# A Mamba scan stage: the C product of every third tile's ninth unit moves from GpSimd to VectorE

## The chip, the cores and the metric

The kernel runs on one core of a Trainium2 chip. The metric is the device time of one execution in microseconds (us). The core has TensorE (PE, whose weight loads are listed apart as PEld), VectorE (DVE), ScalarE (ACT), GpSimd (POOL) and SyncE (SP, which here only issues DMA transfers). The engines run side by side, each through its own list of instructions in order, and wait for each other through counting semaphores.

## The reference

The reference is one layer of a gated cross-attention block whose "attention" is a Mamba selective scan, followed by a mixture of experts. The change touches only the scan. Cut to that:

```python
u = silu(conv(in_proj(ctx)) + conv_b)               # 4 batches x 1024 channels x 1024 times
delta = softplus(dt_proj(x_proj(u)[:32]) + dt_b)
Bm, Cm = ...                                        # 16 states each, shared by all channels
def step(state, xs):                                # over time
    d_t, B_t, C_t, u_t = xs
    dA = exp(d_t[..., None] * A)
    state = state * dA + (d_t * u_t)[..., None] * B_t[:, None, :]
    y_t = einsum('ben,bn->be', state, C_t)
    return state, y_t
y = y + D * u
y = y * silu(layernorm(x))
x = x + tanh(g_xattn) * y
```

After it come the routing of tokens, 32 experts and a shared expert, which the change leaves alone.

## The kernel before

`program` runs five stages one after the other: `mamba_inputs`, `selective_scan`, `shared_pass` (part 0), `experts`, `shared_pass` (part 1). All data is f32.

`selective_scan` works through NU = 32 **channel tiles** (4 batches x 8 tiles of 128 channels; tile i belongs to batch i // 8). A tile has NST = 16 **units**, one for each state n. A unit, numbered k = 16 i + n, is a 128 x 1024 array, channels by time. For one unit each engine does one step, and each walks the 512 units in the same order:

- TensorE, `multiply_b(k)` (L1021, 8 matmuls): delta times u times B into the one PSUM buffer `psb`. It waits until ScalarE has emptied `psb` of unit k-1 (`s_ev`).
- ScalarE, `copy_input` (L951): copies `psb` to SBUF (`dbu`, groups of four units, two groups). It does this three units ahead (AHEAD), right after the exponential of unit k.
- ScalarE (L958): the decay exp(delta * A) into PSUM `da[k % 2]`. It waits until VectorE's scan of unit k-2 is done (`s_scan`, count k-1), since that scan read the same buffer.
- VectorE (L983), `tensor_tensor_scan`: the state over time, from `da` and `dbu` into one of the four slots of `h` in SBUF. It waits for its decay, for all four copies of its group, and until TensorE has read the slot's last content (`s_ys`).
- GpSimd (L1000): multiplies the slot in place by C (`c[:, n]`, one of 16 resident rows), and raises `s_hc`.
- TensorE, `add_state(k)` (L1031, 8 transposing matmuls): adds the product into PSUM `psy`, the tile's sum over the states. In TensorE's list it stands after `multiply_b(k + 6)` (BEHIND). Units 6 to 9 also carry the D * u term (L1040).

When the tile's 16 units are summed, VectorE's `gate_tile` (L975) multiplies `psy` by the gate and by silu. It stands in VectorE's list after the scan of unit 1 of the *next* tile (GATED), and TensorE may begin the next tile's sum only after it (`s_gated`). SyncE stores the result and loads what the following tiles need; at the turn of a batch (tiles 8, 16, 24) it also loads the new B matrices `m0`, `m1` and the 16 rows of C, each behind a wait for the last reader.

VectorE and GpSimd are joined by `s_scan` one way and, through TensorE's transposes and the four slots of `h`, by `s_ys` the other way.

Of the kernel before, what the change touches and what calls it, by code (L numbers as in the profile page):

```python
# [8 lines left out]
DI, NST, DR, DC = 1024, 16, 32, 4  # L9
# [5 lines left out]
ET = DI // P  # L15
# [13 lines left out]
GN = 4  # L29
# [5 lines left out]
ALU = mybir.AluOpType  # L35
# [8 lines left out]
def after(eng, sem, value):  # L44

    if isinstance(value, int):
        if value > 0:
            eng.wait_ge(sem, value)
    else:
        assert value.min_val > 0  # L50
        eng.wait_ge(sem, value)
# [726 lines left out]
def selective_scan(nc, io, dr, ident, arena, m0, duT, early):  # L778
# [4 lines left out]
    with ExitStack() as ctx:  # L783
        sb = lambda name, shape, dt=F32: ctx.enter_context(nc.sbuf_tensor(name, shape, dt))
        sem = Semaphores(nc, ctx)
        NU = B * ET
        SETS = NU * NST
        PARTS = 4
        CP = NC // PARTS
        HR = 4  # L790
        AHEAD, BEHIND = 3, 6
        GATED, SKIPPED = 1, 6
        skip = sb("skip", [P, P])
        gate = sb("gate2", [P, 1])
        m0, m1 = m0[:], sb("m", [P, TB * ROW], F32R)[:]
        m = [v.rearrange("p (t c n) -> p t c n", t=TB, c=NC) for v in (m0, m1)]
        c = sb("c", [P, NST, L])
        ad = sb("ad", [P, 2, NST + 1])
        dl = sb("dl", [P, 2, L])
        dbu = sb("dbu", [P, 2, GN, L])  # L800
        h = sb("h", [P, HR, L])
        aux = sb("aux", [P, ET, P])
        da = [ctx.enter_context(nc.psum_tensor(f"da{i}", [P, L], F32)) for i in range(2)]
# [9 lines left out]
        s_cl = [sem(f"p2_c_loaded{n}") for n in range(NST)]  # L813
# [6 lines left out]
        s_da = sem("p2_decay")  # L820
        s_scan = sem("p2_state")
        s_hc = sem("p2_state_times_c")
        s_ys = sem("p2_summed")
        s_sk = sem("p2_skip_matrix")
        s_skip = sem("p2_skip_added")
# [4 lines left out]
        def units(body):  # L830
            for i in range(NU):
                for n in range(NST):
                    body(i, n, i * NST + n)

        @block.sync
        def _(sp):
# [21 lines left out]
                    sp.dma_start(dst_, src_).then_inc(s_m[half], 16)  # L858

            def load_c(b, n):  # L860
                after(sp, s_hc, (b * ET - 1) * NST + n + 1 if b else 0)
                sp.dma_start(c[:, n], dr["c"][b, n].partition_broadcast(P)).then_inc(s_cl[n], 16)

            def load_u(i):
# [31 lines left out]
            for n in range(3):  # L896
                load_c(0, n)
            load_m(0, 1)
            for n in range(3, NST):
                load_c(0, n)  # L900

            for i in range(NU):
                b = (i + 1) // ET
# [7 lines left out]
                if turned:  # L911
                    for n in range(8, 12):
                        load_c(b, n)
# [55 lines left out]
        @block.vector  # L969
        def _(dve):  # L970
            def gate_tile(i):

                dve.wait_ge(s_szl, i * 16 + 16)
                dve.wait_ge(s_ys, i * NST + NST)
                dve.scalar_tensor_tensor(out=aux[:], in0=psy[:], scalar=gate[:, 0:1], in1=aux[:],  # L975
                                         op0=ALU.mult, op1=ALU.mult).then_inc(s_gated, 1)

            def unit(i, n, k):
                dve.wait_ge(s_da, k + 1)
                dve.wait_ge(s_ev, (k // GN) * GN + GN)  # L980

                after(dve, s_ys, k - HR + 1)
                dve.tensor_tensor_scan(h[:, k % HR, :], da[k % 2][:, :], dbu[:, (k // GN) % 2, k % GN, :], 0.0, ALU.mult,  # L983
                                       ALU.add).then_inc(s_scan, 1)
                if n == GATED and i:
                    gate_tile(i - 1)

            dve.wait_ge(s_gate, 1)
            units(unit)
            gate_tile(NU - 1)  # L990

        @block.gpsimd
        def _(pool):
            pool.memset(f32(m1), 0.0).then_inc(s_zero, 1)

            def unit(i, n, k):
                if i % ET == 0:
                    pool.wait_ge(s_cl[n], (i // ET) * 16 + 16)
                pool.wait_ge(s_scan, k + 1)
                pool.tensor_tensor(h[:, k % HR, :], h[:, k % HR, :], c[:, n, :], ALU.mult).then_inc(s_hc, 1)  # L1000

            units(unit)

        @block.tensor
        def _(pe):
            def multiply_b(k):

                i, g, r = k // NST, (k % NST) // GN, k % GN
                if g == 0:
                    if i:  # L1010
                        pe.wait_ge(s_du[r], i * 64)
                    elif r == 0:
                        pe.wait_ge(early["du"], 64)
                half = k % (ET * NST) // NH
                if k == 0:
                    pe.wait_ge(early["m"], 2 * TB // BAND * 16)
                elif k % (ET * NST) in (0, NH):
                    pe.wait_ge(s_m[half], (i // ET + half) * 2 * TB // BAND * 16)
                after(pe, s_ev, k)
                for j in range(CP):  # L1020
                    mm = pe.matmul(psb[:, j], duT[:, r * CP + j, :], m[g // 2][:, :, r * CP + j, g % 2 * GN:(g % 2 + 1) * GN], start=True, stop=True)  # L1021
                mm.then_inc(s_mm, 1)

            def add_state(k):

                i, n = k // NST, k % NST
                if n == 0:
                    after(pe, s_gated, i)
                pe.wait_ge(s_hc, k + 1)
                for t in range(ET):  # L1030
                    mm = pe.matmul(psy[:, t, :], h[:, k % HR, t * P:(t + 1) * P], ident[:], is_transpose=True,  # L1031
                                   start=(n == 0 and t % 4 == 0), stop=(n == NST - 1 and t % 4 == 3))
                mm.then_inc(s_ys, 1)
                if n == SKIPPED:
                    pe.wait_ge(s_sk, i + 1)
                    pe.wait_ge(s_ut, i * 16 + 16)
                if 0 <= n - SKIPPED < ET // 2:

                    for t in (2 * (n - SKIPPED), 2 * (n - SKIPPED) + 1):
                        mm = pe.matmul(psy[:, t, :], ut[:, t * P:(t + 1) * P], skip[:], start=False, stop=False)  # L1040
                    if n == SKIPPED + ET // 2 - 1:
                        mm.then_inc(s_skip, 1)

            for k in range(SETS + BEHIND):
                if k < SETS:
                    multiply_b(k)
                if k >= BEHIND:
                    add_state(k - BEHIND)
# [968 lines left out]
```

## Time and profile before

| | us |
|---|---|
| time, median of 3 runs | 4216.48 |
| the 3 runs | 4215.31 to 4220.93 |
| the profiled execution, its own time | 4213.03 |
| its span (first to last instruction) | 4211.3 |
| scan stage: first scan to last gate, in the trace | 552.1 to 1785.1 |
| GpSimd busy in the whole span | 1799.1 (43%) |
| VectorE busy | 3031.8 (72%) |
| TensorE busy | 3847.6 (91%) |

Shares of the whole span average over five stages with different limits. The scan stage is some 1233 us, 29% of the span, and in it GpSimd is busy nearly without a break, which the overall 43% hides. The timeline view lists instructions of one engine in order of time and merges equal neighbours into one row; idle time below about 0.15 us inside a row is not printed. Records of neighbouring instructions of VectorE or GpSimd may overlap by up to 0.09 us, so a pace is read from start to start.

### The profile page before, as it was taken

Reading aid. Unit: us, or ns where it says so; the run is one execution under the profiler, and the core shown is the slowest. Engines: PE = TensorE matmul, PEld = TensorE weight load, DVE = VectorE, ACT = ScalarE, POOL = GpSimd, SP = SyncE. Lnnn points to the kernel's source line nnn. Section 1 sums busy time; section 2 is a strip of 40 time slices with the busy share of each in tenths; the row PEclk is TensorE's granted clock in tenths of the full one; section 3 lists DMA queues with packets and bytes.
Section 4 is the critical chain, followed back from the end, with each engine's and each line's share of the span. In section 5 each row is a group of like instructions: output and inputs, shape, how many; then the busy total and the mean of one; then the engine's idle time right before and its main releaser. Section 6 shows DMA issues by size and latency. Waiting matters only on the chain. (4 is left out here: it accounts for less than half of the span.)

```text
span 4211.3 us, 59482 instructions
## 1 busy us (share of the span) xinstructions
PE 3847.6 (91%) x21088; PEld 3151.6 (75%) x21088; DVE 3031.8 (72%) x3701; ACT 2150.4 (51%) x2257; POOL 1799.1 (43%) x1010
## 2 busy tenths in 40 slices
PE   8888378888888888869999989999999999999999
PEld 4444268888778888758888868888888888788887
DVE  7878579999999999867777755555555555455555
ACT  3677678989888889722222234444444444300000
POOL 0355279999999999923333320000000000122221
PEclk9998589999999999979999989999999999999999
DMA  6675753463453553445555557666666666677643
GB/s 231 233 274 224 256 192 108 136 183 116 140 172 116 161 154 113 138 170 175 174 183 184 189 191 245 233 236 232 235 233 234 233 236 238 220 269 262 204 161 121
DMA packets 330294, 821.67 MB, mean 195 GB/s; under 512 B 65872, under 2 KB 111696, under 8 KB 320784
## 3 DMA queue, kind: packets, MB, share of 16 engines
q1 hardware_dynamic: 298240, 752.23, 52.0%
q0 software_dynamic: 31744, 67.23, 5.3%
q8 instruction: 104, 1.70, 0.2%
q14 instruction: 62, 0.51, 0.0%
q10 hardware_dynamic: 144, 0.00, 0.0%
HBM read 603.38 MB, written 245.27 MB: 202 GB/s over the span
## 5 line engine op out<-in xcount | busy, mean ns | idle before, releaser
L1000 POOL TENSOR_TENSOR h<-h,c 128x1024 f32<-128x1024 f32 x512 | 1205.4, 2412 | 33.8 <-DVE h L983 30.8
L983 DVE TENSOR_TENSOR_SCAN h<-da,dbu 128x1024 f32<-128x1024 f32 x512 | 1134.5, 2272 | 67.6 <-ACT dbu L951 51.6
L958 ACT ACTIVATE da<-dl,ad 128x1024 f32<-128x1024 f32 x512 | 588.7, 1150 | 80.7 <-DVE h L983 67.4
L1031 PE MATMUL psy<-ident,h 128*128 128x128 f32 x4096 | 561.4, 281 | 46.1 <-POOL h L1000 26.8
L951 ACT ACTIVATE dbu<-psb 128x1024 f32<-128x1024 f32 x512 | 523.0, 1021 | 61.8 <-PE psb L1021 50.6
L1916 DVE TENSOR_TENSOR wsp<-arena,wsp 128x2048 fp32r<-128x2048 f32 x198 | 447.6, 2288 | 99.9 <-ACT wsp L1869 99.7
L1031 PEld LDWEIGHTS psy<-ident,h 128*128 128x128 f32 x4096 | 446.8, 143 | 79.7 <-POOL h L1000 52.0
L1755 POOL DMA_INDIRECT xg<-scratch_xn,ids x64 | 63.5, 992 | 1034.1 <-PE psT L1773 1010.7
L1869 ACT ACTIVATE wsp<-arena 128x2048 fp32r<-128x2048 f32 x198 | 370.9, 1910 | 24.2 <-DMA arena<-in_w 24.0
L1021 PE MATMUL psb<-m,du_taps 128*128 128x128 f32 x2048 | 288.9, 288 | 62.8 <-ACT dbu L951 62.8
L1021 PE MATMUL psb<-m_first,du_taps 128*128 128x128 f32 x2048 | 292.2, 291 | 47.1 <-ACT dbu L951 22.6
L1021 PEld LDWEIGHTS psb<-m,du_taps 128*128 128x128 f32 x2048 | 251.5, 193 | 99.8 <-ACT dbu L951 94.6
L1021 PEld LDWEIGHTS psb<-m_first,du_taps 128*128 128x128 f32 x2048 | 258.8, 198 | 78.1 <-issue 39.0
L1280 POOL DMA_INDIRECT scratch_tab<-tok_s,si_s x128 | 125.4, 980 | 444.9 <-DVE si_s L1578 398.7
L1442 ACT ACTIVATE hT_s<-psH_s 128x512 fp32r<-128x512 f32 x64 | 38.4, 599 | 503.9 <-PE psH_s L1392 485.5
L426 PE MATMUL psX<-arena 128*128 128x512 f32 x512 | 231.9, 605 | 11.2 <-DMA arena<-in_ctxT 11.2
L759 POOL TENSOR_TENSOR lbuf<-lbuf,ebuf 128x1024 f32<-128x1024 f32 x32 | 75.5, 2361 | 343.3 <-DVE ebuf L693 343.3
L1782 PE MATMUL psO<-wsp,hT 128*128 128x512 f32 x512 | 213.8, 418 | 2.1 <-DVE ob L1927 2.1
L1782 PE MATMUL psG<-wsp,xT_place 128*128 128x512 f32 x512 | 203.0, 397 | 4.9 <-DVE wsp L1916 4.9
L1855 ACT ACTIVATE xT_place<-psT 128x512 fp32r<-128x512 f32 x128 | 76.6, 598 | 250.3 <-PE psT L1773 250.3
L1783 PE MATMUL psO<-wsp,hT 128*128 128x512 f32 x512 | 202.3, 395 | 0.0
L1782 PE MATMUL psU<-wsp,xT_place 128*128 128x512 f32 x512 | 202.3, 395 | 0.0
(208 smaller groups left out, 8100.6 us busy)
## 6 DMA issues: line engine op xcount, KB each, us to landing
arena<-in_w SPq DMA_DIRECT2D x192, 1024.0 KB, 7.1
du_taps<-scratch_duT SPq DMA_DIRECT2D x496, 128.0 KB, 2.9
scratch_duT<-duT SPq DMA_DIRECT2D x64, 512.0 KB, 4.7
c<-scratch_c SPq DMA_DIRECT2D x64, 512.0 KB, 8.6
scratch_xT<-xT_s SPq DMA_DIRECT2D x32, 1024.0 KB, 4.9
scratch_ob<-ob SPq DMA_DIRECT2D x64, 512.0 KB
xT_place<-scratch_xT SPq DMA_DIRECT2D x32, 1024.0 KB, 6.4
xz<-in_x SPq DMA_DIRECT2D x32, 512.0 KB, 5.5
```

Of the source, the lines that this page charges most:

```text
L426: mm = pe.matmul(psX[q % 2][:, hb * HB:(hb + 1) * HB], w_in[:, k, et * P:(et + 1) * P], ctxT[:, b % 2, k, hb * HB:(hb + 1) * HB], start=(k ...
L951: act.activation(dbu[:, g % 2].rearrange("p n (t c) -> p n t c", c=NC)[:, :, :, r * CP:(r + 1) * CP], psb[:].rearrange("p c t n -> p n t c ...
L958: act.activation(da[k % 2][:, :], dl[:, i % 2, :], ACT.Exp, scale=ad[:, i % 2, n:n + 1]).then_inc(s_da, 1)
L983: dve.tensor_tensor_scan(h[:, k % HR, :], da[k % 2][:, :], dbu[:, (k // GN) % 2, k % GN, :], 0.0, ALU.mult, ALU.add).then_inc(s_scan, 1)
L1000: pool.tensor_tensor(h[:, k % HR, :], h[:, k % HR, :], c[:, n, :], ALU.mult).then_inc(s_hc, 1)
L1021: mm = pe.matmul(psb[:, j], duT[:, r * CP + j, :], m[g // 2][:, :, r * CP + j, g % 2 * GN:(g % 2 + 1) * GN], start=True, stop=True)
L1031: mm = pe.matmul(psy[:, t, :], h[:, k % HR, t * P:(t + 1) * P], ident[:], is_transpose=True, start=(n == 0 and t % 4 == 0), stop=(n == NST ...
L1280: pool.indirect_dma_start(dr["tab"], bass.IndirectOffsetOnAxis(ap=si[:, par, k:k + 1], axis=0), tok[:, par:par + 1], None, bounds_check=NE ...
L1782: pe.matmul(dst, l[0], r[0], start=(k == 0), stop=False)
L1783: pe.matmul(dst, l[0], r[1], start=False, stop=False)
L1869: act.activation(wsp[:, slot, 0, halves[half]], raw[:, c, halves[half]], ACT.Copy).then_inc(s_whi, 1)
L1916: dve.tensor_tensor(wsp[:, slot, 1, halves[half]], raw[:, c, halves[half]], f32(wsp[:, slot, 0, halves[half]]), ALU.subtract).then_inc(s_w ...
```

## The change

In tiles i with i % 3 = 1 (1, 4, 7, ..., 31: eleven tiles) unit n = 8 is treated differently. Its scan writes the states back to `da[k % 2]` in PSUM instead of to `h`; VectorE then waits for its own scan (`s_hs`), multiplies by C into the slot of `h`, waits for that product (`s_hd`) and only then counts `s_scan`. GpSimd skips the unit. TensorE's `add_state` and SyncE's `load_c` wait for `s_hd` or `s_hc`, whichever stands for the unit, by `product_done`. Nothing else is changed: 501 products are left on GpSimd, 11 are on VectorE.

```diff
+        SHARED, THIRD = 8, 3
+        def by_dve(k):
+            return k % NST == SHARED and (k // NST) % THIRD == 1
+        by_pool = [0]
+        for k in range(SETS):
+            by_pool.append(by_pool[-1] + (not by_dve(k)))
+        def product_done(eng, k):
+            if by_dve(k):
+                eng.wait_ge(s_hd, k + 1 - by_pool[k])
+            else:
+                eng.wait_ge(s_hc, by_pool[k + 1])
...
             def load_c(b, n):
-                after(sp, s_hc, (b * ET - 1) * NST + n + 1 if b else 0)
+                if b:
+                    product_done(sp, (b * ET - 1) * NST + n)
...
-                after(dve, s_ys, k - HR + 1)
-                dve.tensor_tensor_scan(h[:, k % HR, :], da[k % 2][:, :], dbu[:, (k // GN) % 2, k % GN, :], 0.0, ALU.mult,
-                                       ALU.add).then_inc(s_scan, 1)
+                if by_dve(k):
+                    j = k + 1 - by_pool[k]
+                    dve.tensor_tensor_scan(da[k % 2][:, :], da[k % 2][:, :], dbu[:, (k // GN) % 2, k % GN, :], 0.0,
+                                           ALU.mult, ALU.add).then_inc(s_hs, 1)
+                    dve.wait_ge(s_cl[n], (i // ET) * 16 + 16)
+                    after(dve, s_ys, k - HR + 1)
+                    dve.wait_ge(s_hs, j)
+                    dve.tensor_tensor(h[:, k % HR, :], da[k % 2][:, :], c[:, n, :], ALU.mult).then_inc(s_hd, 1)
+                    dve.wait_ge(s_hd, j)
+                    dve.sem_inc(s_scan, 1)
+                else:
+                    after(dve, s_ys, k - HR + 1)
+                    dve.tensor_tensor_scan(h[:, k % HR, :], da[k % 2][:, :], dbu[:, (k // GN) % 2, k % GN, :], 0.0, ALU.mult,
+                                           ALU.add).then_inc(s_scan, 1)
...
-                pool.wait_ge(s_scan, k + 1)
-                pool.tensor_tensor(h[:, k % HR, :], h[:, k % HR, :], c[:, n, :], ALU.mult).then_inc(s_hc, 1)
+                if not by_dve(k):
+                    pool.wait_ge(s_scan, k + 1)
+                    pool.tensor_tensor(h[:, k % HR, :], h[:, k % HR, :], c[:, n, :], ALU.mult).then_inc(s_hc, 1)
...
-                pe.wait_ge(s_hc, k + 1)
+                product_done(pe, k)
```

VectorE's list at the start of the scan stage, before (L983 is a scan, L975 a gate; x16 is sixteen in a row):

```order
L983 SCALAR_TENSOR_TENSOR h<-da,dbu 128x1024 x18
L975 SCALAR_TENSOR_TENSOR aux<-psy,gate,aux 128x1024
L983 SCALAR_TENSOR_TENSOR h<-da,dbu 128x1024 x16
L975 SCALAR_TENSOR_TENSOR aux<-psy,gate,aux 128x1024
L983 SCALAR_TENSOR_TENSOR h<-da,dbu 128x1024 x16
```

and in the changed kernel, in the same place (L1015 is the scan, L995 the gate, L1005 the scan into PSUM, L1010 the product):

```order
L1015 SCALAR_TENSOR_TENSOR h<-da,dbu 128x1024 x18
L995 SCALAR_TENSOR_TENSOR aux<-psy,gate,aux 128x1024
L1015 SCALAR_TENSOR_TENSOR h<-da,dbu 128x1024 x6
L1005 SCALAR_TENSOR_TENSOR da<-da,dbu 128x1024
L1010 TENSOR_TENSOR h<-da,c 128x1024
L1015 SCALAR_TENSOR_TENSOR h<-da,dbu 128x1024 x9
L995 SCALAR_TENSOR_TENSOR aux<-psy,gate,aux 128x1024
```

After the gate of tile 0, VectorE scans units 2 to 7 of tile 1, then unit 8 with its product, then nine scans (9 to 15, and 0 and 1 of tile 2), then the gate. Only the product is new; no other row of VectorE's list has moved, and the lists of ScalarE, TensorE and SyncE hold the same instructions in the same order.

## Rows read from the trace of the kernel before

**Rows 1.** Page, costliest groups: busy us, mean ns, idle before and its releaser

```profile
L1000 POOL TENSOR_TENSOR h<-h,c 128x1024 f32<-128x1024 f32 x512 | 1205.4, 2412 | 33.8 <-DVE h L983 30.8
L983 DVE TENSOR_TENSOR_SCAN h<-da,dbu 128x1024 f32<-128x1024 f32 x512 | 1134.5, 2272 | 67.6 <-ACT dbu L951 51.6
L958 ACT ACTIVATE da<-dl,ad 128x1024 f32<-128x1024 f32 x512 | 588.7, 1150 | 80.7 <-DVE h L983 67.4
...
L951 ACT ACTIVATE dbu<-psb 128x1024 f32<-128x1024 f32 x512 | 523.0, 1021 | 61.8 <-PE psb L1021 50.6
```

**Rows 2.** Windows view, scan stage: busy PE, PEld, DVE, ACT, POOL; PEclk, DMA share, GB/s

```profile
553.00:1785.00 1232.00, 1092.38 (x8669) 991.63 (x8668) 1171.32 (x544) 1085.22 (x1051) 1205.39 (x512) 0.98 0.46 142
```

**Rows 3.** Windows view from one gate's start to the next, tiles 4 and 13

```profile
709.90:748.18 38.28, 34.17 (x271) 31.54 (x270) 36.58 (x18) 33.52 (x33) 37.74 (x17) 0.96 0.36 111
...
1056.58:1094.35 37.77, 33.80 (x274) 30.60 (x274) 36.63 (x18) 34.14 (x34) 37.63 (x17) 1.00 0.36 112
```

**Rows 4.** Timeline of VectorE, tile 13: start, us, instruction, [idle before <-releaser]

```profile
1056.58 1.28 DVE L975 SCALAR_TENSOR_TENSOR aux<-psy,gate,aux 128x1024 f32<-128x1024 f32 x1 [0.45 <-PE psy L1031]
...
1071.23 8.83 DVE L983 TENSOR_TENSOR_SCAN h<-da,dbu 128x1024 f32<-128x1024 f32 x4
1080.22 8.83 DVE L983 TENSOR_TENSOR_SCAN h<-da,dbu 128x1024 f32<-128x1024 f32 x4 [0.16 <-ACT dbu L951]
1089.45 4.47 DVE L983 TENSOR_TENSOR_SCAN h<-da,dbu 128x1024 f32<-128x1024 f32 x2 [0.40 <-ACT dbu L951]
1094.35 1.28 DVE L975 SCALAR_TENSOR_TENSOR aux<-psy,gate,aux 128x1024 f32<-128x1024 f32 x1 [0.43 <-PE psy L1031]
```

**Rows 5.** Timeline of VectorE: the scans of units 2 and 9, tile 13

```profile
1057.78 2.28 DVE L983 TENSOR_TENSOR_SCAN h<-da,dbu 128x1024 f32<-128x1024 f32 x1
...
1073.43 2.27 DVE L983 TENSOR_TENSOR_SCAN h<-da,dbu 128x1024 f32<-128x1024 f32 x1
```

**Rows 6.** Timeline of POOL: 22 products in a row; units 2, 8, 9 of tile 13

```profile
1038.81 51.92 POOL L1000 TENSOR_TENSOR h<-h,c 128x1024 f32<-128x1024 f32 x22
...
1060.14 2.36 POOL L1000 TENSOR_TENSOR h<-h,c 128x1024 f32<-128x1024 f32 x1
...
1074.18 2.44 POOL L1000 TENSOR_TENSOR h<-h,c 128x1024 f32<-128x1024 f32 x1
...
1076.55 2.43 POOL L1000 TENSOR_TENSOR h<-h,c 128x1024 f32<-128x1024 f32 x1
```

**Rows 7.** Timeline of VectorE, tile 4, gate to gate

```profile
709.90 1.28 DVE L975 SCALAR_TENSOR_TENSOR aux<-psy,gate,aux 128x1024 f32<-128x1024 f32 x1 [0.48 <-PE psy L1031]
...
725.63 17.81 DVE L983 TENSOR_TENSOR_SCAN h<-da,dbu 128x1024 f32<-128x1024 f32 x8 [1.20 <-ACT dbu L951]
743.79 4.47 DVE L983 TENSOR_TENSOR_SCAN h<-da,dbu 128x1024 f32<-128x1024 f32 x2 [0.35 <-ACT dbu L951]
748.18 1.26 DVE L975 SCALAR_TENSOR_TENSOR aux<-psy,gate,aux 128x1024 f32<-128x1024 f32 x1
```

**Rows 8.** Lines view, VectorE in the first stage: busy us, mean ns | idle before

```profile
L677 DVE SCALAR_TENSOR_TENSOR u<-psX,conv_w,u 128x1023 f32<-128x1023 f32 x32 | 41.0, 1283 | 1.1
...
L693 DVE TENSOR_TENSOR ebuf<-ebuf,cbuf 128x1024 f32<-128x1024 f32 x32 | 39.2, 1225 | 1.1
...
L698 DVE TENSOR_TENSOR duT<-psV,duT 128x1024 fp32r<-128x1024 f32 x19 | 23.2, 1222 | 35.5 <-ACT duT L567 35.0 <-DMA scratch_duT<-duT 0.4
...
L653 DVE BATCH_NORM_AGGREGATE mv<-stats 128x2 f32<-128x12 f32 x32 | 6.7, 209 | 4.7 <-DVE stats L648 0.2
```

**Rows 9.** Timeline of VectorE, batch turn: tile 7, units 14 and 15

```profile
854.60 2.29 DVE L983 TENSOR_TENSOR_SCAN h<-da,dbu 128x1024 f32<-128x1024 f32 x1 [2.85 <-ACT da L958]
857.73 2.29 DVE L983 TENSOR_TENSOR_SCAN h<-da,dbu 128x1024 f32<-128x1024 f32 x1 [0.84 <-ACT da L958]
```

**Rows 10.** Timeline of SyncE's DMA issues, same turn

```profile
840.75 10.66 SPq L848 DMA_DIRECT2D du_taps<-scratch_duT  x16
```

**Rows 11.** Timeline of VectorE, the stage's last gate

```profile
1783.84 1.28 DVE L975 SCALAR_TENSOR_TENSOR aux<-psy,gate,aux 128x1024 f32<-128x1024 f32 x1 [5.05 <-PE psy L1031]
```

More of the change, by code:

```diff
@@ L822, in selective_scan @@
         s_hc = sem("p2_state_times_c")
+        s_hs = sem("p2_state_in_psum")
+        s_hd = sem("p2_state_times_c_on_dve")
         s_ys = sem("p2_summed")
```

## The prediction, on record before the changed kernel ran

> **What bounds the kernel now.** I read the windows view of the scan stage first, since nothing else changes. Of 1232 us GpSimd is busy 1205, VectorE 1171, TensorE 1092, ScalarE 1085 [rows 2]. GpSimd's products wait only 33.8 us in total, VectorE's scans 67.6 us [rows 1]. So GpSimd leads, but by 34 us in 1232: the question is whether VectorE has room for what is put on it.
>
> Then I read one ordinary tile on both engines, gate to gate. 22 products in a row take 51.92 us, 2.36 us each [rows 6], so 16 take 37.76 us, and the tile takes 37.77 [rows 3]. GpSimd paces it. But VectorE is hardly slower: at the end of the tile it waits 0.43 us before the gate [rows 4]. And the two run on each other's heels: after the gate VectorE's scan of unit 2 ends at 1057.78 + 2.28 = 1060.06 [rows 5] and GpSimd starts unit 2 at 1060.14, 0.08 us later [rows 6]. From there VectorE gains slowly: unit 9's scan ends at 1075.70 [rows 5] and its product starts at 1076.55 [rows 6], 0.85 us later. That is the whole stock in front of GpSimd at the place of the change, although `h` has four slots. It can't grow over several tiles, because the gate (VectorE) waits for TensorE's last transpose, which waits for GpSimd's unit 15: each tile starts again from 0.08.
>
> **A rehearsal in the trace.** In tile 4 the scan of unit 8 came late for a reason of its own: it waited 1.20 us for a ScalarE copy [rows 7]. It started 725.63 - 709.90 = 15.73 us after the gate, against 1071.23 - 1056.58 = 14.65 in tile 13 [rows 4]: VectorE was 1.08 us late at exactly the unit that the change touches. The gate-to-gate time was 38.28 in place of 37.77, so 0.51 of the 1.08 came through and 0.57 was absorbed (by the 0.43 before the gate, the 0.08 by which records overlap, and ends of the waits for copies). At the end the gate followed the scans with no wait [rows 7]: VectorE had become the bound of that tile. Four tiles are of this kind (4, 9, 19, 26; 38.25 to 38.29 us each), and they are those with a granted clock of 0.96 in place of 1.00, tile 4 against tile 13 in [rows 3]: a short stretch at the lower of the two levels (1.2 in place of 2.4 GHz). So VectorE's own need for a tile is 38.28 - 1.08 = 37.20 us, and a delay d at unit 8 gives 37.20 + d once d is above 0.57.
>
> **The change, part by part.** *Removed from GpSimd:* 11 products of 2.36 us, 26.0 us. *Added to VectorE,* per changed tile, the delay d of unit 9's scan:
> - The scan of unit 8 now ends before anything follows. A scan's record is 2.27 to 2.29 us, but the step from scan to scan is (8.83 - 2.27) / 3 = 2.19 [rows 4]. The overlap that is lost is 0.09.
> - The wait of the product for its own engine: L677 depends each time on the instruction before it and stands idle 1.1 us in 32 times, 0.03 each [rows 8].
> - The product, one PSUM and one SBUF input: L698 has just this form, 1.22 us [rows 8].
> - The wait for the product, then the semaphore count, then the next scan: L653 stands behind the same pair (own wait, count) and idles 4.7 / 32 = 0.15 [rows 8].
>
> d = 0.09 + 0.03 + 1.22 + 0.15 = 1.49. A scan that writes PSUM isn't in the trace. Nearest are the two products with input from PSUM and from SBUF, 1.22 against 1.23 [rows 8], so the side of a memory seems to cost VectorE nothing; I take 0, and for the bounds plus or minus 0.13, what ScalarE's two 128x1024 activations into PSUM and out of it differ by (1.15 and 1.02 [rows 1]). With 1.28 for the product (L677) as an upper price, d lies between 1.2 and 1.7.
>
> *Moved waits.* ScalarE's exponential of unit 10 waits for `s_scan` of unit 8, now 1.4 us later, but it takes 1.15 us [rows 1] while VectorE needs 2.2 for the scan of unit 9, so it is in time; it and the copy behind it keep their distance to VectorE. TensorE gets product 8 earlier than before. The product's waits for C and for a free slot are long met: it is no tighter than the scan's wait for the same slot was. SyncE waits on products only at batch turns.
>
> *Ordinary changed tile.* By VectorE: 37.20 + 1.49 = 38.69. By GpSimd: unit 9 can start at 1075.70 + 1.49 + 0.08 = 1077.27, which is 0.72 later than the 1076.55 of now, although unit 8 (2.37 us) is gone: GpSimd stands idle 3.1 us. From there its seven products are as before, so 37.77 + 0.72 = 38.49. The larger counts: 38.69 - 37.77 = **+0.92 us**. The time taken from GpSimd buys nothing, since nothing lies ready for it. Tiles 1, 10, 13, 16, 22, 25, 28: 7 x 0.92 = 6.44.
>
> *Tiles 4 and 19.* They are bound by VectorE already, so all of d shows: 2 x 1.49 = 2.98. If the low-clock stretches fall in other tiles the sum is 9 x 0.92 instead, 1.1 less.
>
> *Tile 7.* Before the turn VectorE waits 2.85 us at unit 14 and 0.84 at unit 15 [rows 9], for ScalarE, which stands behind TensorE and the transfers for tile 8. These are issued from 840.75 in one go of 10.66 us [rows 10], by waits that lie before unit 8's product or are outlasted by SyncE's own pace. The 1.49 us disappear in the 2.85: 0. What hides them is the turn's transfers; were they faster, this tile would cost 0.92 too.
>
> *Tile 31.* The last gate waits 5.05 us for TensorE [rows 11], so here the path goes by GpSimd: 0.72.
>
> Sum: 6.44 + 2.98 + 0 + 0.72 = 10.1 us. Against the profiled execution (4213.0) this is 4223.1; the median of the runs is 3.5 above it, and I forecast that: 4216.5 + 10.1 = **4226.6**. With d = 1.2 the sum is 7 x 0.63 + 2.4 + 0.4 = 7.2; with d = 1.7 it is 7 x 1.13 + 3.4 + 0.9 = 12.2.
>
> **Rivals.**
> *VectorE's waits for itself are free.* Then d is the product alone, 1.22, and the sum 7 x 0.65 + 2.44 + 0.45 = 7.4: 4223.9, within 0.2%. For it: the idle time behind an own wait is only 0.03. Against it: that engine's steps do overlap when nothing waits (2.19 against 2.27), and the count costs 0.15 in L653. The Trainium skill ("VectorE: DVE Perf Modes", section on the DRAIN that can't be avoided) states that a semaphore between two VectorE instructions costs nothing extra, since the next one waits for the pipe in any case. By that rule the time is this rival's 4223.9; the trace disagrees by about 0.1 us a wait. Chance 0.08.
> *GpSimd's saving comes through (the other side).* If GpSimd always had a product waiting, 11 x 2.36 = 26 us would go: 4190.5. It decides at unit 9 of each changed tile: the stock must cover d, so the 0.85 us there would have to be over 1.49 and then some. And VectorE must afford it: over three tiles it needs 2 x 37.20 + 38.69 = 113.1 against 113.3 now, so even a perfect stock buys 0.2 us in three tiles unless the waits for copies (0.16 and 0.40 [rows 4]) go as well. In tile 4, where GpSimd did not hold anyone up, the one before unit 0 was still 0.35 [rows 7]. Chance 0.03.
> *The clock.* Each changed tile has TensorE idle some 1.5 us longer, next to which a low-clock stretch could follow. One makes TensorE's group of eight matmuls late and VectorE by 1.08 [rows 3, 7]. In all ten VectorE-bound tiles that is 10.8 more: 4237. For it: four tiles had one with no such extra idle time. Against it: the other 24 away from the batch turns did not. Chance 0.06; one or two such stretches more or fewer belong to my forecast.
> *That the change does not do what it says:* VectorE's list has the product, GpSimd's has 501, so I give it none.
>
> **How the numbers follow.** Forecast 0.80, free waits 0.08, saving comes through 0.03, clock 0.06; 0.03 is left for surprises of a scan into PSUM, a third of it a gain. The range takes in d from 1.2 to 1.7 (7.2 to 12.2), a stretch or two of low clock fewer or more (-1 to +2), and the runs' own scatter of some 2 us: 4220.5 to 4233. A measurement of this kernel can tell about 0.2%, 8.4 us, from no change. The forecast's 10.1 lies only 1.7 above it, so a quarter of its chance (0.20) falls within: same 0.20 + 0.08 + 0.02 = 0.30, slower 0.66, faster 0.04.
>
> **What would show it.** In the changed kernel's trace: gate-to-gate 38.6 to 38.8 us in ordinary changed tiles with no wait before the gate, 37.8 in the others; GpSimd's busy time down 26 us and its idle time up by some 35, about 3 us of it before unit 9's product; the scan of unit 9 starting 3.7 us after that of unit 8; tile 7 unchanged. I am wrong if changed tiles take 37.8 or less, if GpSimd has no idle time before unit 9, or if a scan into PSUM takes clearly other than 2.27 us.

## The result, and the profile after

| | before | changed |
|---|---|---|
| median of the runs, us | 4215.9 (4211.8 to 4221.6, 8 runs) | 4228.1 (4224.5 to 4234.8, 8 runs) |
| ratio | | 1.0027, 95% interval 1.0016 to 1.0038 |
| profiled execution, span | 4211.3 | 4223.9 |
| first scan to last gate's end, in the trace | 1233.0 | 1246.8 |

The changed kernel is slower by 12 us (7 to 16 by the interval). The forecast was 10.1 us slower. In the traces the whole difference lies in the scan stage; what follows the last gate takes 2426 us in both. The interval covers 10.1 as well as 12, so the time alone can't tell whether the terms of the sum were right: the trace has to. Each ratio here and below is worked out from the single runs with its interval, and can differ from the quotient of the two medians by up to 0.0012; where they differ, the text goes by the ratio.

The two groups that answer to [rows 1], from the page of the changed kernel (busy us, mean ns, idle before and its releaser):

```profile
L1033 POOL TENSOR_TENSOR h<-h,c 128x1024 f32<-128x1024 f32 x501 | 1180.8, 2406 | 72.3 <-DVE h L1015 70.5
L1015 DVE TENSOR_TENSOR_SCAN h<-da,dbu 128x1024 f32<-128x1024 f32 x501 | 1110.6, 2272 | 65.6 <-ACT dbu L971 43.4
```

GpSimd has 24.6 us less to do than in [rows 1] and waits 38.5 us more. Tile 13 shows where, in VectorE's timeline (the changed counterpart of [rows 4]):

```profile
1060.29 1.28 DVE L995 SCALAR_TENSOR_TENSOR aux<-psy,gate,aux 128x1024 f32<-128x1024 f32 x1 [0.44 <-PE psy L1064]
1061.49 13.29 DVE L1015 TENSOR_TENSOR_SCAN h<-da,dbu 128x1024 f32<-128x1024 f32 x6
1074.95 2.30 DVE L1005 TENSOR_TENSOR_SCAN da<-da,dbu 128x1024 f32<-128x1024 f32 x1 [0.16 <-ACT dbu L971]
1077.38 1.23 DVE L1010 TENSOR_TENSOR h<-da,c 128x1024 f32<-128x1024 f32 x1
1078.85 15.55 DVE L1015 TENSOR_TENSOR_SCAN h<-da,dbu 128x1024 f32<-128x1024 f32 x7 [0.24 <-DVE h L1010]
1094.75 4.47 DVE L1015 TENSOR_TENSOR_SCAN h<-da,dbu 128x1024 f32<-128x1024 f32 x2 [0.35 <-ACT dbu L971]
1099.14 1.26 DVE L995 SCALAR_TENSOR_TENSOR aux<-psy,gate,aux 128x1024 f32<-128x1024 f32 x1
```

From gate to gate it is 1099.14 - 1060.29 = 38.85 us, against 37.77 in [rows 4], and the second gate has no wait before it: VectorE bounds the tile. From the scan of unit 8 to that of unit 9 it takes 1078.85 - 1074.95 = 3.90 us; an ordinary step there is 2.21. So d, the delay of unit 9's scan, is 1.69. VectorE's own time for the tile isn't all work: it holds the waits for ScalarE's copies that are left (0.16 and 0.35 here). GpSimd's timeline of the same tile:

```profile
1059.01 18.97 POOL L1033 TENSOR_TENSOR h<-h,c 128x1024 f32<-128x1024 f32 x8
1081.22 21.29 POOL L1033 TENSOR_TENSOR h<-h,c 128x1024 f32<-128x1024 f32 x9 [3.24 <-DVE h L1015]
```

It ends unit 7, has nothing for 3.24 us, and starts unit 9 0.08 us after that scan's end.

Gate to gate, the changed tiles 1, 10, 13, 16, 22 and 28 take 38.84 to 38.94 us (before 37.77 to 37.82), tile 4 38.85 (38.28), tiles 19 and 25, which now have a low-clock stretch, 39.77 and 39.93 (38.27 and 37.74), the last one 0.9 more. Against before these nine and tile 31 together are 11.6 us longer, in the profiled execution of the changed kernel and again in that of its repetition below. The whole scan stage is 13.8 us longer in the one and 9.5 in the other; the tiles around the batch turns make most of that difference.

### The profile page after: what moved, and what is told of

Its sections match the earlier page's. It is cut to its first block and busy times, and to the rows that moved or that the text cites. A ratio compares the mean times of both kernels' runs of the same rounds, so it can differ in the third digit from the quotient of the medians.

```text
span 4223.9 us, 59503 instructions
## 1 busy us (share of the span) xinstructions
PE 3839.8 (91%) x21088; PEld 3142.3 (74%) x21088; DVE 3047.3 (72%) x3712; ACT 2149.7 (51%) x2257; POOL 1774.3 (42%) x999
## 5 line engine op out<-in xcount | busy, mean ns | idle before, releaser
L1033 POOL TENSOR_TENSOR h<-h,c 128x1024 f32<-128x1024 f32 x501 | 1180.8, 2406 | 72.3 <-DVE h L1015 70.5
L1015 DVE TENSOR_TENSOR_SCAN h<-da,dbu 128x1024 f32<-128x1024 f32 x501 | 1110.6, 2272 | 65.6 <-ACT dbu L971 43.4
```

## Experiments

Six kernels ask why the change costs what it does, five whether a share of GpSimd's products can be moved for less. Where the text says "before", it means runs of the kernel before on the same chip. Gate-to-gate times are read from the starts of the gates in each trace.

### GpSimd gets its load back

```diff
-                if not by_dve(k):
+                if by_dve(k):
+                    for half in range(2):
+                        pool.wait_ge(s_sp, 2 * (k - by_pool[k]) + half + 1)
+                        pool.tensor_tensor(spare[:], spare[:], spare[:], ALU.mult).then_inc(s_sp, 1)
+                else:
```

> The changed kernel, but GpSimd gets its load back: in each of the 11 units it multiplies a spare 128x512 tile by itself twice (about 2.4 us), waiting for nobody; nothing reads the result. Theory (VectorE bounds the changed tiles, GpSimd idles 3.2 us before unit 9 anyway): the same time as the changed kernel, 12 us over before, gate to gate 38.85 us, GpSimd's idle time before unit 9 down to about 0.8 us. Rival (the relief of GpSimd is worth something and the loss would be larger without it): up to 2.4 us more for each of 10 tiles, 30 us or more over before.

Measured: 4225.6 us against 4217.8, ratio 1.0010 (0.9999 to 1.0020). Ordinary changed tiles take 38.83 to 38.86 us, as in the changed kernel's repetition below. GpSimd's timeline in one of them:

```profile
1057.97 28.42 POOL L1040 TENSOR_TENSOR h<-h,c 128x1024 f32<-128x1024 f32 x12
1086.30 2.22 POOL L1037 TENSOR_TENSOR spare<-spare 128x512 f32<-128x512 f32 x2
1089.59 21.22 POOL L1040 TENSOR_TENSOR h<-h,c 128x1024 f32<-128x1024 f32 x9 [1.07 <-DVE h L1017]
```

The load, 2.2 us, goes into the 3.2 us of idle time and the next product starts when it did. So what GpSimd is spared in the changed kernel is worth nothing there. The times read somewhat less than for the changed kernel (the intervals overlap from 1.0016 to 1.0020; the tiles give no reason for it), and at most 8 us over before, not the rival's 30.

### The product at unit 0 in place of unit 8

```diff
-        SHARED, THIRD = 8, 3
+        SHARED, THIRD = 0, 3
```

> The changed kernel with unit 0 in place of unit 8 (same eleven tiles), where GpSimd is 1.3 us behind VectorE and not 0.85, and where VectorE waits soon after for the gate. Theory (VectorE's own sum for the tile counts, wherever the product stands): gate to gate 38.85 us in the stretch that holds the product, 10 to 12 us over before. Rival (the short stock in front of GpSimd at unit 8 decides): with the longer stock and the wait before the gate the product costs little, 0 to 4 us over before, or below it.

Measured: 4235.2 against 4217.8, ratio 1.0031 (1.0020 to 1.0042). The product at unit 0 of tile i stands ahead of the gate of tile i - 1, so in the counting used above it lengthens tile i - 1 (3, 6, 9, ..., 30). The rows are the end of tile 12:

```profile
1063.34 2.30 DVE L1005 TENSOR_TENSOR_SCAN da<-da,dbu 128x1024 f32<-128x1024 f32 x1 [0.36 <-ACT dbu L971]
1065.77 1.23 DVE L1010 TENSOR_TENSOR h<-da,c 128x1024 f32<-128x1024 f32 x1
1067.24 2.29 DVE L1015 TENSOR_TENSOR_SCAN h<-da,dbu 128x1024 f32<-128x1024 f32 x1 [0.24 <-DVE h L1010]
1069.44 1.26 DVE L995 SCALAR_TENSOR_TENSOR aux<-psy,gate,aux 128x1024 f32<-128x1024 f32 x1
```

The step is the same 3.90 us and the gate again has no wait. In the three that no low clock disturbs (tiles 3, 24 and 30) it is 39.0 to 39.1 us, 0.15 to 0.25 over the 38.85 of the theory. The rival, cheaper where GpSimd's stock is longer, falls. But six others (tiles 6, 9, 12, 18, 21 and 27) take 40.0 to 40.4, and the tile after the product mostly 38.2. These are stretches with a low clock, by the mark of the prediction: unit 8's scan starts some 15.7 us after the gate in place of 14.6. Before, 4 tiles had one; here it is 17 of 31, most in pairs: the tile that holds the product (37.16 + 1.69 + 1.08 = 39.93) and the one behind it. The windows view of the scan stage has a granted clock of 0.95, where [rows 2] has 0.98 and the changed kernel 0.99:

```profile
557.00:1811.00 1254.00, 1114.97 (x8672) 1020.62 (x8672) 1185.90 (x555) 1084.02 (x1051) 1181.14 (x501) 0.95 0.46 140
```

TensorE's idle time at the product and that around the gate lie side by side in this kernel. That this brings the low clock is suggested by the place alone, and is not shown; why it also comes in the stretch ahead of the product was not settled. I had missed it in what I expected of this run; it is the clock rival of the prediction, at another place.

### Half the product, and the product twice

```diff
-                    dve.tensor_tensor(h[:, k % HR, :], da[k % 2][:, :], c[:, n, :], ALU.mult).then_inc(s_hd, 1)
+                    dve.tensor_tensor(h[:, k % HR, 0:L // 2], da[k % 2][:, 0:L // 2], c[:, n, 0:L // 2], ALU.mult).then_inc(s_hd, 1)
```

> The changed kernel, but VectorE's product covers only 512 of the 1024 columns in the 11 units (the other half is left unmultiplied and stale). The delay d falls from 1.69 by 0.53 us. Theory (cost of a tile is d less 0.61): gate to gate 38.3 us, 6 to 8 us over before. Rival (a fixed cost of the scan into PSUM or of the extra waits, not VectorE's time): 11 to 12 us over before, as with the whole product.

```diff
-                    dve.wait_ge(s_hs, j)
+                    dve.wait_ge(s_hs, 2 * j - 1)
+                    dve.tensor_tensor(h[:, k % HR, :], da[k % 2][:, :], c[:, n, :], ALU.mult).then_inc(s_hs, 1)
+                    dve.wait_ge(s_hs, 2 * j)
```

> The changed kernel, but VectorE does the product of the 11 units twice, with a wait for the first between. d grows by 1.22 + 0.13 = 1.35 us to 3.04. Theory: each changed tile grows by all of it, gate to gate 40.2 us, 25 to 28 us over before (tile 7 begins to show too). Rival (fixed cost): 12 to 15 us over before.

Half: 4221.1 against 4217.8, ratio 1.0002 (0.9992 to 1.0012). Twice: 4253.3 against 4217.8, ratio 1.0077 (1.0059 to 1.0095). VectorE's timeline of tile 13, half:

```profile
1064.43 1.28 DVE L995 SCALAR_TENSOR_TENSOR aux<-psy,gate,aux 128x1024 f32<-128x1024 f32 x1 [0.43 <-PE psy L1064]
...
1081.53 0.70 DVE L1010 TENSOR_TENSOR h<-da,c 128x512 f32<-128x512 f32 x1
...
1102.78 1.26 DVE L995 SCALAR_TENSOR_TENSOR aux<-psy,gate,aux 128x1024 f32<-128x1024 f32 x1
```

and twice:

```profile
1070.86 1.28 DVE L995 SCALAR_TENSOR_TENSOR aux<-psy,gate,aux 128x1024 f32<-128x1024 f32 x1 [0.42 <-PE psy L1066]
...
1087.95 1.23 DVE L1010 TENSOR_TENSOR h<-da,c 128x1024 f32<-128x1024 f32 x1
1089.21 1.23 DVE L1012 TENSOR_TENSOR h<-da,c 128x1024 f32<-128x1024 f32 x1
...
1110.96 1.26 DVE L995 SCALAR_TENSOR_TENSOR aux<-psy,gate,aux 128x1024 f32<-128x1024 f32 x1
```

| kernel | step 8 to 9 | d | gate to gate | less d |
|---|---|---|---|---|
| half | 3.37 | 1.16 | 38.30 to 38.35 | 37.14 |
| changed | 3.90 | 1.69 | 38.85 | 37.16 |
| twice | 5.16 | 2.95 | 40.10 | 37.15 |

The tile is VectorE's own 37.15 us plus d, over the whole range: the slope is one. The fixed-cost rival falls. The total for the half, 1 us by the ratio and 5 at most, is below the 6 to 8 that I expected. Nine tiles at 0.54 are 4.9 us, so the tiles as measured fit the upper bound only; fewer low-clock stretches don't explain it in the kept trace, which has five (before: four). This miss stays open. The total for twice is some 5 us above the top of what I expected: in this execution tiles 4, 16, 19, 25 and 31 took 41.4 to 42.8 us. In tile 4 a low-clock stretch stands right behind the long pause at unit 8; TensorE's timeline there, and the windows view of the same place (the third number from the end is the granted clock):

```profile
740.92 1.97 PE L1056 MATMUL psb<-m,du_taps 128*128 128x128 f32 x8 [2.46 <-ACT dbu L971]
742.69 1.93 PE L1066 MATMUL psy<-ident,h 128*128 128x128 f32 x8
...
749.27 1.06 PE L1066 MATMUL psy<-ident,h 128*128 128x128 f32 x8
...
740.90:745.00 4.10, 4.08 (x19) 4.08 (x20) 4.10 (x3) 3.15 (x3) 3.67 (x2) 0.50 0.19 60
```

After 2.46 us without work its groups of eight take 1.9 us in place of 1.1, at a granted clock of 0.50 (the lower level, 1.2 GHz), then come back. In tiles 10 and 28 TensorE stands idle for 2.46 us at the same place and the clock stays at 1.00, so the length of this pause alone doesn't decide.

### The batch turns

```diff
-            return k % NST == SHARED and (k // NST) % THIRD == 1
+            return k % NST == SHARED and (k // NST) % ET == ET - 1 and k // NST < NU - 1
```

> VectorE's product only in unit 8 of tiles 7, 15 and 23, the three before a batch turn. Theory of the prediction (VectorE's wait at units 14 and 15 hides it): the same as before within 1 us. Rival (the later scans push ScalarE's and TensorE's steps and with them the transfers, as the longer tiles 7 and 8 of the changed kernel suggest): each turn 1 to 2.3 us longer, 3 to 7 us over before.

Measured: 4213.8 against 4215.6, ratio 0.9999 (0.9990 to 1.0008). VectorE's timeline of tile 7:

```profile
846.17 1.23 DVE L1010 TENSOR_TENSOR h<-da,c 128x1024 f32<-128x1024 f32 x1
847.64 11.19 DVE L1015 TENSOR_TENSOR_SCAN h<-da,dbu 128x1024 f32<-128x1024 f32 x5 [0.24 <-DVE h L1010]
859.83 4.59 DVE L1015 TENSOR_TENSOR_SCAN h<-da,dbu 128x1024 f32<-128x1024 f32 x2 [1.00 <-ACT da L978]
865.72 4.47 DVE L1015 TENSOR_TENSOR_SCAN h<-da,dbu 128x1024 f32<-128x1024 f32 x2 [1.31 <-ACT dbu L971]
```

The wait at unit 14 is 1.00 here and was 2.85 in [rows 9], which would fit a product paid out of it, but the two traces don't show that: in the changed kernel, with the same product in tile 7, the wait is 2.90. What counts is the time. Three products before three turns cost -4 to +3 us in all, so a turn costs -1.4 to +1.1. Of the rival's 1 to 2.3 a turn all but the lowest value is out. The turn itself varies more than that: tile 7 took 40.7 to 44.9 us in the seven executions with VectorE's product in it (once half, once twice), and tiles 7 and 8 together 78.9 to 83.7; in the six others, four of which move a share of 32 to 192 columns there, it was 40.6 to 43.6 and 79.7 to 85.2.

### The changed kernel again

> The changed kernel once more, beside the three below: 12 us over before (1.003). Ordinary changed tiles 38.85 us gate to gate. The turn after tile 7 and the tiles with a low-clock stretch show how far they scatter from one execution to the next.

Measured, beside the runs of this and the next two: 4228.3 against 4215.6, ratio 1.0027 (1.0017 to 1.0037). Ordinary tiles 38.83 to 38.86 us. Tiles 10 and 31 have the low-clock stretch here, where 19 and 25 had it; tile 7 took 40.72 us in place of 43.81.

### The product one scan later, from SBUF

```diff
+                after(dve, s_ys, k - HR + 1)
+                dve.tensor_tensor_scan(h[:, k % HR, :], da[k % 2][:, :], dbu[:, (k // GN) % 2, k % GN, :], 0.0, ALU.mult,
+                                       ALU.add).then_inc(s_scan, 1)
+                if k and by_dve(k - 1):
+                    dve.wait_ge(s_cl[n - 1], (i // ET) * 16 + 16)
+                    dve.wait_ge(s_scan, k)
+                    dve.tensor_tensor(h[:, (k - 1) % HR, :], h[:, (k - 1) % HR, :], c[:, n - 1, :], ALU.mult).then_inc(s_hd, 1)
```

> The same eleven units, but the scan writes to its slot of h as before and VectorE multiplies it there one scan later (after the scan of unit 9), so that nothing waits for the scan just issued and the next scan doesn't wait for the product. Theory (the loss is VectorE's time, 0.5 us of which is waits for itself): d falls from 1.69 to about 1.15, gate to gate 38.3 us, 6 to 7 us over before. Rival (two inputs from SBUF in place of one hinder GpSimd, which then works on another slot): GpSimd's products beside it take longer than 2.4 us and the tile is 38.6 us or more.

Measured: 4220.0 against 4215.6, ratio 1.0011 (1.0002 to 1.0020). Gate to gate 38.14 to 38.19 us, and 38.5 in tiles 4 and 19, where unit 8's scan came some 0.35 us late (at a granted clock of 1.00; not traced). In VectorE's timeline the product follows the scan with no gap and the next scan follows the product so:

```profile
1070.60 4.47 DVE L1003 TENSOR_TENSOR_SCAN h<-da,dbu 128x1024 f32<-128x1024 f32 x2 [0.15 <-issue]
1074.98 1.20 DVE L1009 TENSOR_TENSOR h<-h,c 128x1024 f32<-128x1024 f32 x1
1076.10 13.30 DVE L1003 TENSOR_TENSOR_SCAN h<-da,dbu 128x1024 f32<-128x1024 f32 x6
```

d is 1076.10 - 1074.98 = 1.12, so the rest of the 1.69 us, 0.57, is what the waits for itself cost VectorE: idle time of 0.13 and 0.24, and the overlap of 0.08 to 0.09 with the neighbouring instruction that is lost on either side of the product (the product's record is 0.03 shorter here too). GpSimd's timeline beside it:

```profile
1075.15 5.68 POOL L1026 TENSOR_TENSOR h<-h,c 128x1024 f32<-128x1024 f32 x2 [1.52 <-DVE h L1003]
```

Two products in 5.68 us in place of 4.7: the first, which starts 0.17 us after VectorE's, takes 3.2 to 3.3 us in the 11 cases, longer by about the time that VectorE's still runs. GpSimd had been idle for 1.52 us (its unit 8 is gone), so here VectorE never came second. With the input from PSUM, in the changed kernel, GpSimd's product beside VectorE's took its usual 2.4, and VectorE's 1.23 us, in the tiles where GpSimd was busy as in tiles 19 and 25, where it wasn't. So both theory and rival hold in part: the tile is the cheaper one, and the two engines do hinder each other.

### A share of 192 columns in every tile, from SBUF, and of 32

```diff
+                if n == SHARED + 1:
+                    dve.wait_ge(s_cl[SHARED], (i // ET) * 16 + 16)
+                    dve.wait_ge(s_scan, k)
+                    dve.tensor_tensor(h[:, (k - 1) % HR, 0:CUT], h[:, (k - 1) % HR, 0:CUT], c[:, SHARED, 0:CUT], ALU.mult).then_inc(s_hd, 1)
...
-                pool.tensor_tensor(h[:, k % HR, :], h[:, k % HR, :], c[:, n, :], ALU.mult).then_inc(s_hc, 1)
+                cut = CUT if n == SHARED else 0
+                pool.tensor_tensor(h[:, k % HR, cut:], h[:, k % HR, cut:], c[:, n, cut:], ALU.mult).then_inc(s_hc, 1)
```

> The kernel before, with a small share moved in every tile: of unit 8 VectorE multiplies the first 192 of 1024 columns one scan later, GpSimd the other 832. Theory: VectorE needs 37.20 + 0.26 = 37.46 us a tile, GpSimd 37.76 less 0.44 = 37.32, so gate to gate 37.45 in place of 37.77 in some 24 tiles, 6 to 8 us below before less 0.26 in tiles with a low-clock stretch. Rival (a product on VectorE costs more than its columns say, by waits, or the balance moves the low-clock stretches): 0 to 5 us over before.

Measured: 4243.0 against 4215.6, ratio 1.0072 (1.0053 to 1.0090). The theory falls: tiles take 37.77 us, and eight of them some 41. The loss lies in those eight. The lines of VectorE and GpSimd around the product, first in an ordinary tile, then in a long one:

```profile
1280.51 0.82 DVE L992 TENSOR_TENSOR h<-h,c 128x192 f32<-128x192 f32 x1
...
1281.04 2.55 POOL L1009 TENSOR_TENSOR h<-h,c 128x1024 f32<-128x1024 f32 x1
...
1318.29 3.14 DVE L992 TENSOR_TENSOR h<-h,c 128x192 f32<-128x192 f32 x1
...
1318.87 2.34 POOL L1009 TENSOR_TENSOR h<-h,c 128x1024 f32<-128x1024 f32 x1
```

In both, VectorE starts while GpSimd is in its product of unit 8 (it ends at 1281.09 and at 1318.90). In the first it gets in behind that product, and GpSimd's next one takes 2.55 us in place of 2.40; in the second it waits for the next one as well, to 1321.2. The two take turns, an instruction at a time; which comes next varied from tile to tile, and no run shows why. 192 columns cost VectorE 0.79 to 0.85 us in 23 of the 32 cases and 3.05 to 3.23 in nine. The long case comes with a second loss: d is about 3.1 there, which gives 40.1 us, and in all eight tiles of some 41 the granted clock is 0.96 or less.

With 32 columns (`CUT = 32`):

> The split with both inputs from SBUF, with 32 columns for VectorE in place of 192. Theory (VectorE's product waits until GpSimd's running product ends): it still takes 0.6 us or more, in some tiles about 3, and the step from unit 9 to 10 stays at 2.7 us or more, with 5 in some tiles. Rival (time by columns): the product takes 0.2 us, the step is 2.3 us, and the time is that of before.

Measured: 4248.0 against 4218.3, ratio 1.0078 (1.0063 to 1.0092). All instances of the product:

```profile
L992 DVE TENSOR_TENSOR h<-h,c x32: 852/1026/3380, 584.4 to 1794.6; 128x32 f32<-128x32 f32 x32
```

(shortest, median and longest in ns.) A sixth of the columns takes no less time: it isn't the columns that cost. In the ordinary tiles VectorE's product ends some 0.05 us after GpSimd's product of unit 8, with 192 columns some 0.22 us after it; it takes longer with 32 because GpSimd's share is the larger one (992 columns, 2.33 us, in place of 832, 1.97). Here 11 of the 32 take about 3.3 us.

### The same share with one input from PSUM

```diff
-                    dve.tensor_tensor(h[:, (k - 1) % HR, 0:CUT], h[:, (k - 1) % HR, 0:CUT], c[:, SHARED, 0:CUT], ALU.mult).then_inc(s_hd, 1)
+                    dve.tensor_tensor(h[:, (k - 1) % HR, 0:CUT], da[k % 2][:, 0:CUT], c[:, SHARED, 0:CUT], ALU.mult).then_inc(s_scan, 1)
```

> As the split of 192 columns, but VectorE's product takes its first input from PSUM (the decay of unit 9, not the states of unit 8, so these 192 columns are wrong in every tile) and only C from SBUF; it counts the scan of unit 9. Theory (with two inputs from SBUF VectorE and GpSimd can't work at once, and that made the split cost 30 us; with one they can): the product takes 0.35 us whatever GpSimd does, the step from unit 9 to 10 is 2.55 us and never 5, gate to gate 37.5 us in place of 37.77, 5 to 8 us below before. Rival (any product on VectorE there costs 0.8 us and now and then 3): 25 to 30 us over before, as with both inputs from SBUF.

Measured: 4201.5 against 4218.3, ratio 0.9972 (0.9960 to 0.9983).

```profile
L991 DVE TENSOR_TENSOR h<-da,c x32: 332/332/333, 577.7 to 1755.5; 128x192 f32<-128x192 f32 x32
```

All 32 products take 0.33 us. The step from unit 9 to 10 is 2.43 against 2.18 without a product, d is 0.25, and most tiles take 37.33 to 37.47 us: VectorE's 37.15 + 0.25 = 37.40 again. In every tile GpSimd is in its product of unit 8 when VectorE's starts, 1.3 to 1.5 us into it as in the split from SBUF, and still in it when VectorE's ends. What this kernel also changes, that unit 9 is counted only after the product, holds up nobody, for GpSimd isn't done with unit 8 by then. So the input is the cause of the two before: a product of VectorE with two inputs from SBUF doesn't run beside a product of GpSimd (0.79 to 3.23 us for 192 columns); with one it does (0.33). The Trainium skill says so ("SBUF — State Buffer", section "SBUF: two separate sides"): VectorE's second port pair is shared with GpSimd, and an instruction of VectorE with two inputs from SBUF holds it alone against one of GpSimd that reads SBUF. The traces agree: 3.2 to 3.3 us for GpSimd's product where VectorE's from SBUF came first, 0.8 to 3.4 for VectorE's where GpSimd's came first, and no delay for either with one input from PSUM.

The total, 12 us below before by the ratio (7 to 17), is more than the 5 to 8 expected. Away from the turns 24 tiles save 0.37 us each, and the four that had a low-clock stretch before save 0.88, since no tile of this trace has one: 12.4 us.

### The share from PSUM, with the unit's scan cut in two

```diff
+                if n == SHARED:
+                    dve.tensor_tensor_scan(da[k % 2][:, 0:CUT], da[k % 2][:, 0:CUT], dbu[:, (k // GN) % 2, k % GN, 0:CUT], 0.0,
+                                           ALU.mult, ALU.add).then_inc(s_hs, 1)
+                    dve.wait_ge(s_cl[n], (i // ET) * 16 + 16)
+                    dve.wait_ge(s_hs, i + 1)
+                    dve.tensor_tensor_scan(h[:, k % HR, CUT:], da[k % 2][:, CUT:], dbu[:, (k // GN) % 2, k % GN, CUT:],
+                                           da[k % 2][:, CUT - 1:CUT], ALU.mult, ALU.add)
+                    dve.tensor_tensor(h[:, k % HR, 0:CUT], da[k % 2][:, 0:CUT], c[:, n, 0:CUT], ALU.mult).then_inc(s_scan, 1)
```

> A kernel that could beat both: in every tile the scan of unit 8 is cut in two, its first 160 columns into PSUM, the other 864 into h (starting from the last state in PSUM, for which it must wait), and VectorE multiplies the 160 from PSUM right behind; GpSimd multiplies the 864. Everything is computed. Theory: d is the second scan's start and the wait for the first (0.16 + 0.13) plus 0.22 for the product, about 0.5, so VectorE needs 37.15 + 0.5 = 37.65 us and GpSimd 37.4: gate to gate 37.65 in place of 37.77, 3 to 5 us below before. Rival (a scan that starts from a state costs more than that, or a later scan wakes the low-clock stretches): 37.9 us and more, 3 us or more over before.

Measured: 4211.3 against 4216.3, ratio 0.9985 (0.9976 to 0.9994): below before by 2 to 10 us, and below the changed kernel. One tile of VectorE:

```profile
1063.92 1.26 DVE L979 SCALAR_TENSOR_TENSOR aux<-psy,gate,aux 128x1024 f32<-128x1024 f32 x1
...
1078.53 0.50 DVE L988 TENSOR_TENSOR_SCAN da<-da,dbu 128x160 f32<-128x160 f32 x1
1079.14 2.02 DVE L992 TENSOR_TENSOR_SCAN h<-da,dbu 128x864 f32<-128x864 f32 x1
1081.08 0.30 DVE L994 TENSOR_TENSOR h<-da,c 128x160 f32<-128x160 f32 x1
1081.29 15.58 DVE L996 TENSOR_TENSOR_SCAN h<-da,dbu 128x1024 f32<-128x1024 f32 x7
...
1101.61 1.27 DVE L979 SCALAR_TENSOR_TENSOR aux<-psy,gate,aux 128x1024 f32<-128x1024 f32 x1
```

d is 2.76 - 2.21 = 0.55, the tile 37.69 us, 37.65 to 37.72 in all tiles away from the turns, as expected. None of these tiles has the longer time that a low-clock stretch gave four tiles of before (38.3). Of what these tiles save, 24 x 0.08 = 1.9 us is the moved share and 4 x 0.59 = 2.4 us the absence of such stretches, which one trace doesn't show to be lasting. The kept trace is that of the slowest of the eleven executions: its scan stage takes 1234.4 us, 1.4 more than before, because tiles 7, 8, 15, 16 and 23 around the turns took 6.0 us more in all. So that the kernel is faster is shown by the runs, and that its ordinary tiles are shorter by the trace; whether it costs anything at the turns is open.

## Why the prediction was right, point by point

- **What bounds a tile.** Right. VectorE's own time was worked out as 37.20 us from one disturbed tile of the trace before; five kernels with d from 0.25 to 2.95 give 37.14 to 37.16. The three with both inputs of the product from SBUF give 37.03 to 37.04 (38.16 - 1.12, 37.77 - 0.74, 37.97 - 0.94); some 0.06 of that difference is a shorter wait for a copy before unit 12, the rest was not traced. The late scan in tile 4 was a good rehearsal, since it hit the same unit.
- **The relief of GpSimd buys nothing.** Right: forecast 3.1 us of idle time before unit 9, measured 3.2, and with its load put back the tiles don't change.
- **d, the term that was mis-sized.** Forecast 1.49, measured 1.69. The lost overlap (0.09) and the product (1.23) were right, and a scan into PSUM takes 2.30 us against 2.29 for one that starts fresh into `h`, so the unknown operation cost nothing. The two waits of VectorE for itself were too cheap: behind the scan 0.13, not 0.03; behind the product, with the count, 0.24, not 0.15. The rows that I took them from (L677 and L653) are of other pairs of instructions: between the two products of the kernel with twice the work, where an elementwise operation waits for another as in L677, the idle time is 0.03 (1087.95 + 1.23 = 1089.18, then 1089.21). With 1.69 an ordinary tile is 37.16 + 1.69 = 38.85, 1.07 over before in place of 0.92.
- **The sum: partly luck.** The prediction's sum for d = 1.7 is 12.2 us and the tiles measured 11.6, but not by its terms. It gave tiles 4 and 19 all of d (3.4 us together), since they had the low-clock stretches before; the stretches came elsewhere, and the two cost 0.57 + 1.50 (0.55 + 0.57 in the repetition). By the prediction's other reading, all nine tiles alike, it is 9 x 1.07 + 0.91 = 10.5. The missing 1.1 is the clock: before had two low-clock stretches in these ten tiles (4 and 19), at 0.5 us each; the changed kernel has two as well (19 and 25, in the repetition 10 and 31), at about 1.1 each, since VectorE bounds the tile now and all of the delay shows.
- **Free waits.** Out by the trace: the idle times of 0.13 and 0.24 us are there, and taking both waits away with the lost overlaps gave 0.57 us of 1.69 back. The second idle time stands behind a wait and a count, and no run parts the two. What the Trainium skill states ("VectorE: DVE Perf Modes", section on the DRAIN that can't be avoided), that a semaphore between two VectorE instructions costs nothing extra, doesn't hold for these pairs; even between two elementwise products, where 0.03 us is idle, the overlap of 0.08 us is lost.
- **Tile 7 hides its product.** Right within what can be told (-1.4 to +1.1 us a turn). I had argued that the transfers end at the same time whatever the product does; in single executions they don't, the turn varies by 4 us by itself, and in the changed kernel's trace tile 7 is 0.7 us and tile 8 1.6 us longer than before.
- **Tile 31.** Forecast 0.72, measured 0.91: the same term d.
- **The clock.** By the late scan of unit 8 the changed kernel has three low-clock stretches (tiles 3, 19 and 25) and its repetition two (10 and 31), against four before, so the forecast's bounds held. All of them stand ahead of unit 8, as before; TensorE is idle for 1.2 us at the product, and in the nine changed tiles away from the turns and the stage's end none follows it. But the rival was real for other kernels: with the product next to the gate, or with a pause of TensorE of 2.1 to 2.8 us at the product (twice the work, and the long tiles of the splits from SBUF), they came in more tiles, and cost 0.8 to 2.7 us each. What decides between the pauses that bring one and those that don't was not settled. The price put on this rival, ten VectorE-bound tiles at 1.08, was too high by the prediction's own count: nine are bound by VectorE, and two of them already had a stretch.
- **The other side.** It failed at the point named: GpSimd's stock of 0.85 us at unit 9 is under d. And at unit 0, where the stock is longer, VectorE's time bounded the tile all the same.

## What to carry to other kernels

When two engines share a loop nearly evenly, work out for each the time that it alone needs for one round (here 37.2 and 37.8 us) and add no more to the one than the difference: 0.25 us on VectorE in every round gained 0.37 us a round (in a kernel whose moved share isn't the right product), 0.55 gained 0.08, and 1.69 lost 1.07. A disturbed round in the trace tells the other engine's need without a run: find one where it was late and see how much came through. And count an instruction that waits for its own engine's last result by what the whole chain costs (1.69 us here), not by its record (1.23).

## What the runs showed of the hardware that I had not expected

- VectorE's elementwise product with both inputs from SBUF and GpSimd's product exclude each other, an instruction at a time: 32 columns took 0.85 to 3.4 us, and a GpSimd product of 2.4 us took 3.3 beside a VectorE product of 1.2. With one input from PSUM both run at full pace (0.332 us for 192 columns, 32 times out of 32, each beside a product of GpSimd).
- What VectorE loses by waiting for its own last instruction goes by the pair: idle time of 0.03 us between two products, 0.13 from a scan to a product, 0.24 from a product by way of a count to a scan, and in each case the overlap of 0.08 us.
- A scan from a state in PSUM over 864 columns takes 2.02 us and one over 160 columns 0.50: cutting a scan in two costs 0.34 us with its wait (1081.08 - 1078.53 = 2.55 against 2.21).
